# Second attention: row scaling on ScalarE, weight scaling on GpSimd, in place of one VectorE step

## The reference, cut to what matters

```
def _dyn_quant(x):
    s = jnp.maximum(jnp.max(jnp.abs(x), axis=-1, keepdims=True) / 127.0, EPS)
    q = jnp.clip(jnp.round(x / s), -127.0, 127.0)
    return (q, s)
def _w8a8_linear(x, w, b):
    qx, sx = _dyn_quant(x)
    qw, sw = _quant_weight(w)
    y = jnp.einsum('bnc,oc->bno', qx, qw) * (sx * sw[:, 0])
    return y + b
...
q = _w8a8_linear(x, wq, bq) ...
attn = jax.nn.softmax(scores, axis=-1)
o = jnp.einsum('bhnl,bhld->bhnd', attn, v)
return _w8a8_linear(o, wo, bo)
...
x = x + jnp.tanh(g_xattn[1]) * _L1_xattn_ref(_layernorm(x, axis=-1), ctx_2048, ...)
x = x + jnp.tanh(g_ffn[1]) * _L1_ffn_ref(_layernorm(x, axis=-1), ...)
```

## Time and profile before

| | before |
|---|---|
| median of 3 runs | 1870.31 us |
| range of the runs | 1869.5 to 1870.43 us |
| the profiled execution's own time | 1871.33 us |
| its span in the trace | 1869.5 us |
| PE busy | 1741.5 us (93%) |
| DVE busy | 1181.8 us (63%) |
| ACT busy | 1038.8 us (56%) |
| POOL busy | 975.1 us (52%) |

### The profile page before, as it was taken

The page is one execution under the profiler, slowest core; times in us unless marked ns, Lnnn a source line. Parts: engine busy times, 40 slices in busy tenths (PEclk is TensorE's granted clock), DMA queues, the critical chain, the costliest instruction groups (busy, mean ns, idle before and its releaser), DMA issues. The chain is left out here.

```text
span 1869.5 us, 28380 instructions
## 1 busy us (share of the span) xinstructions
PE 1741.5 (93%) x10015; PEld 1355.0 (72%) x10052; DVE 1181.8 (63%) x2415; ACT 1038.8 (56%) x2334; POOL 975.1 (52%) x864
## 2 busy tenths in 40 slices
PE   6999999999999999999998999989999778879997
PEld 4777887777877778777775888879999556634443
DVE  5666555557556776567766657634334678868885
ACT  3566666655655555545554422146665367767875
POOL 5644565445654456545541100048888356657774
PEclk9999999999999999999999999999999889999999
DMA  7111111111111111012122100167889660000000
GB/s 250 48 54 51 51 36 57 55 24 51 36 41 45 51 48 50 19 32 56 53 85 92 63 23 23 45 231 209 227 247 273 160 142 1 1 7 18 24 23 23
DMA packets 113611, 141.36 MB, mean 76 GB/s; under 512 B 38000, under 2 KB 68720, under 8 KB 113280
## 3 DMA queue, kind: packets, MB, share of 16 engines
q1 hardware_dynamic: 106304, 122.76, 21.0%
q0 software_dynamic: 7168, 16.78, 4.3%
HBM read 104.91 MB, written 29.36 MB: 72 GB/s over the span
## 5 line engine op out<-in xcount | busy, mean ns | idle before, releaser
L787 POOL TENSOR_TENSOR a_xcl<-xT,a_xch 128x512 fp32r<-128x512 f32 x64 | 87.3, 1365 | 323.4 <-ACT a_xch L571 323.4
L689 DVE TENSOR_REDUCE a_nmax<-a_S 128x1 f32<-128x192 f32 (+3 forms) x256 | 135.5, 549 | 83.0 <-PE a_S L897 82.8
L954 PE MATMUL a_A<-a_pT,a_vf 128*128 128x512 f32 x320 | 168.0, 607 | 6.5 <-ACT a_pT L592 6.5
L577 ACT ACTIVATE a_pr_odd<-a_S,a_nmax 128x320 f32<-128x320 f32 (+1 forms) x128 | 80.6, 631 | 149.9 <-DVE a_nmax L689 149.8
L120 PE MATMUL a_A<-a_wlo,a_xch 128*128 128x512 f32 x256 | 143.9, 562 | 14.0 <-DVE a_qb L750 11.4
L577 ACT ACTIVATE a_pr_even<-a_S,a_nmax 128x192 f32<-128x192 f32 (+1 forms) x128 | 67.0, 526 | 123.7 <-DVE a_nmax L689 123.4
L120 PE MATMUL a_S<-xl,xh 128*128 128x288 f32 (+3 forms) x320 | 121.8, 381 | 9.7 <-DVE xl L732 5.0
L1612 POOL TENSOR_TENSOR e_wlo<-expert_raw,e_whi 128x1408 fp32r<-128x1408 f32 x31 | 100.3, 3235 | 50.2 <-ACT e_whi L1784 48.0
L2528 PE MATMUL f_HH<-w12T,f_f_xqT 128*128 128x512 bf16 x496 | 117.5, 383 | 6.9 <-DVE f_h L2384 3.8
L714 DVE RECIPROCAL a_rec<-a_rs 128x1 f32<-128x1 f32 x256 | 41.2, 161 | 120.1 <-ACT a_pr_odd L577 67.1
L120 PE MATMUL e_GUP<-e_xgl,e_whi 128*128 128x256 f32 (+1 forms) x384 | 110.4, 287 | 4.3 <-DVE e_xgl L1840 2.7
(11 more groups left out here) (417 smaller groups left out, 5593.9 us busy)
## 6 DMA issues: line engine op xcount, KB each, us to landing
a_pw<-in_L_ffn_w_dram SPq DMA_DIRECT2D x96, 256.0 KB, 2.8
expert_raw<-in_L_ffn_w_gate_dram SPq DMA_DIRECT2D x16, 704.0 KB, 8.1
expert_raw<-in_L_ffn_w_up_dram SPq DMA_DIRECT2D x16, 704.0 KB, 9.9
expert_raw<-in_L_ffn_w_down_dram SPq DMA_DIRECT2D x16, 512.0 KB, 10.3
tern<-a_tern SPq DMA_DIRECT2D x48, 128.0 KB, 1.8
x_res<-in_x_dram SPq DMA_DIRECT2D x4, 1024.0 KB, 9.2
a_raw<-in_L_xattn_wq_dram SPq DMA_DIRECT2D x4, 1024.0 KB, 6.1
a_raw<-in_L_xattn_wo_dram SPq DMA_DIRECT2D x4, 1024.0 KB, 5.5
```

Source lines behind the costliest of these rows:

```text
L577: act.activation(pr[s % 2][:, i, 0:keys(s)], pair(s, i), ACT.Exp, bias=nmax[:, s % 2, i:i + 1], accum_out=rs[:, s % 2, i:i + 1]).then_inc( ...
L689: ve.tensor_reduce(nmax[:, s % 2, i:i + 1], pair(s, i), AX.X, ALU.max, negate=True).then_inc(s_max, 1)
L787: pool.tensor_tensor(xcl[:, t % 2], xT[:, :, tok(t)], xch[:, t % 2].bitcast(F32), ALU.subtract).then_inc(xlo_ready, 1)
L954: pe.matmul(bank, vf[:, par(t), i], pT[:, i % 2], start=i == 0, stop=False)
```

## The change

The step Y leaves the DVE. Its two factors are applied apart: ACT reads the bank QY and multiplies by the row scale `so` into y (new step Y of ACT), and POOL multiplies y by `gsw` just ahead of the addition to x (both in step A). ACT runs Y at the head of a slot, for tile t-3, where DVE ran it near the end of slot t-1 for the same tile; A moves from tile t-2 to tile t-3. PE, when it wants the bank QY, now waits for ACT's read (`y_scaled`). DVE's N waits for `y_scaled` of an older tile before it overwrites `so`, and the feed-forward layer's b waits for `x_done` of its tile.

```diff
-    ACT_ORDER = "q0 t0 i0 t1 c0 v0 k0 e0 O0"
+    ACT_ORDER = "Y0 q0 t0 i0 t1 c0 v0 k0 e0 O0"
-    DVE_ORDER = "D0 o0 M0 b0 x0 N0 Y0 m0"
+    DVE_ORDER = "D0 o0 M0 b0 x0 N0 m0"
...
-             "POOL": {"B": 2, "p": 3, "s": 0, "A": -2}}
+             "POOL": {"B": 2, "p": 3, "s": 0, "A": -3}}
...
-                16: "t0.15 fs0.0 t1.15 fq0.1 fq1.1 fs1.0 fz0.0 O0.15 fs2.0 fz1.0 fs3.0 fz2.0 fc0.2 fv0.2 fz3.0 fa0.0"}
+                16: "Y0.13 t0.15 fs0.0 t1.15 Y0.14 fq0.1 fq1.1 fs1.0 fz0.0 O0.15 fs2.0 fz1.0 fs3.0 fz2.0 Y0.15 fc0.2 fv0.2 fz3.0 fa0.0"}
...
-                 16: "A0.14 fh0.0 fh1.0 fy0.2 fh2.0 fy1.2 fh3.0 A0.15 ft0.0 fp0.2"}
+                 16: "A0.13 fh0.0 A0.14 fh1.0 fy0.2 fh2.0 fy1.2 fh3.0 A0.15 ft0.0 fp0.2"}
...
                     if name == "A":
+                        pool.wait_ge(y_scaled, s + 1)
+                        pool.tensor_tensor(y[:, u], y[:, u], gsw[:], ALU.mult).then_inc(y_ready, 1)
                         pool.wait_ge(y_ready, s + 1)
                         pool.wait_ge(biased, s + 1)
                         pool.tensor_tensor(x[:, s], x[:, s], y[:, u], ALU.add).then_inc(x_done, 1)
...
+                    if name == "Y":
+                        act.wait_ge(y_full, s + 1)
+                        if s > 1:
+                            act.wait_ge(x_done, s - 1)
+                        act.activation(y[:, u], QY[:], ACT.Identity, scale=so[:, u]).then_inc(y_scaled, 1)
...
+                        if s > 1:
+                            ve.wait_ge(y_scaled, s - 1)
                         link(ve.tensor_scalar(so[:, u], amo[:, u:u + 1], 1.0 / 127.0, FLOOR, ALU.mult, ALU.max))
...
-                    if name == "Y":
-                        ve.wait_ge(y_full, s + 1)
-                        if s > 1:
-                            ve.wait_ge(x_done, s - 1)
-                        ve.scalar_tensor_tensor(y[:, u], QY[:], so[:, u], gsw[:], ALU.mult, ALU.mult).then_inc(y_ready, 1)
...
+                        ve.wait_ge(x_done, s + 1)
                         link(ve.bn_stats(f_stats[:, u], x[:, s]))
...
-                        pe.wait_ge(qs_ready if name == "Q" else y_ready, s + 1)
+                        pe.wait_ge(qs_ready if name == "Q" else y_scaled, s + 1)
```

More of the change, by code:

```diff
@@ L2032, in attention1_ffn1_stage @@
                16: "U0.14 P0.15 Y0.14 P1.15 V0.15 fP1.0 V1.15 fT0.1 fP2.0 U0.15 fP3.0 Y0.15"}
-    ACT_JOIN = {10: "q0.12 t0.9 i0.11 t1.9 c0.13 v0.13 k0.11 G0.0 e0.10 O0.9",
[6 rows of a table removed]
-    DVE_JOIN = {13: "D0.13 o0.11 M0.13 fb0.0 x0.15 N0.12 Y0.11",
[3 rows of a table removed]
-    POOL_JOIN = {13: "B0.15 s0.13 fy0.0 A0.11 fy1.0 fp0.0",
-                 14: "s0.14 fy0.1 A0.12 fy1.1 fp0.1",
-                 15: "s0.15 A0.13",
-                 16: "A0.14 fh0.0 fh1.0 fy0.2 fh2.0 fy1.2 fh3.0 A0.15 ft0.0 fp0.2"}
+    ACT_JOIN = {10: "Y0.7 q0.12 t0.9 i0.11 t1.9 c0.13 v0.13 k0.11 G0.0 e0.10 O0.9",
[6 rows of a table added]
+    DVE_JOIN = {13: "D0.13 o0.11 M0.13 fb0.0 x0.15 N0.12",
+                14: "D0.14 o0.12 M0.14 fb0.1 N0.13 fm0.0",
+                15: "D0.15 o0.13 M0.15 fx0.0 N0.14 fm0.1",
+                16: "o0.14 fg0.0 fg1.0 N0.15 fx0.1 fg2.0 o0.15 fb0.2 fg3.0 fH0.0 fH1.0"}
+    POOL_JOIN = {13: "B0.15 s0.13 fy0.0 A0.10 fy1.0 fp0.0",
+                 14: "s0.14 fy0.1 A0.11 fy1.1 fp0.1",
+                 15: "s0.15 A0.12",
+                 16: "A0.13 fh0.0 A0.14 fh1.0 fy0.2 fh2.0 fy1.2 fh3.0 A0.15 ft0.0 fp0.2"}
     HALF = H1 // 4
@@ L2103, in attention1_ffn1_stage @@
             "q_full", "qs_ready", "q_turned", "q_copied", "sc_full", "sc_read", "max_ready", "centred", "exp_done"))
-        p_turned, p_copied, o_full, o_ready, oq_ready, oq_turned, oq_copied, y_full, y_ready = (s_.sem(n) for n in (
-            "p_turned", "p_copied", "o_full", "o_ready", "oq_ready", "oq_turned", "oq_copied", "y_full", "y_ready"))
+        p_turned, p_copied, o_full, o_ready, oq_ready, oq_turned, oq_copied, y_full, y_scaled, y_ready = (s_.sem(n) for n in (
+            "p_turned", "p_copied", "o_full", "o_ready", "oq_ready", "oq_turned", "oq_copied", "y_full", "y_scaled", "y_ready"))
         biased, x_done, turned = s_.sem("biased"), s_.sem("x_done"), s_.sem("turned")
@@ L2547, in feed @@
                         else:
-                            pe.wait_ge(y_ready, NT)
+                            pe.wait_ge(y_scaled, NT)
                         for k in range(F1 // P):
```

## The result

| | before | after |
|---|---|---|
| median | 1870.12 us (18 runs) | 1872.62 us (18 runs) |
| range of the runs | 1868.74 to 1874.98 us | 1871.64 to 1876.0 us |
| ratio to before, 95% interval | | 1.0016 [1.0009, 1.0023] |
| the profiled execution's own time, its span | 1871.33, 1869.5 us | 1872.6, 1870.8 us |
| the D of slot 3 to the end of the span | 338.96 us | 342.41 us |

The changed kernel is slower by 0.16%: 2.5 us above the kernel before, 3.4 us above the forecast of 1869.2, and 0.3 us beyond the upper end of the range. It is inside the 0.2% that I had called "no change" and beside the sign that I had given it.

A forecast was written before the change was run, and what follows sets the result against it. Plain slots were bound by a ring of waits through DVE's m, then by one through S. Terms -2.5 - 0.4 + 0.58 + 1.22 = -1.1 us gave 1869.2 us against the median 1870.31; range 1866.9 to 1872.3.

The forecast's parts named there:

- seven plain slots: Slots 3 to 9: period falls to 8.03 us, gain 0.36 us each, -2.5 us in all.
- slots 10 to 14: Five slots where the read's 0.58 us is exposed and m's 0.66 saved: -0.08 us each, -0.4 in all.
- the read ahead of c: Slot 16, ACT's read of tile 15: delays c of feed-forward tile 2 and POOL's last block, +0.58 us.
- the product ahead of t: Slot 16, POOL's product of tile 15 ahead of the powers: not covered by idle time, +1.22 us.
- the old ring without Y: Plain slots, chain of waits through m, q, t0, P1 and N: 8.39 - 0.66 = 7.73 us, no longer the longest.
- rival C: Slots 2 to 14: full 0.66 us saved in each, 8.6 us, join costs 1.8, total 1863.5; chance 0.05.
- rival A: Plain slots gain nothing because ACT closes them: 1872.1 us; chance 0.15.
- the shift: Plain slots: q starts 0.05 us after the next D; taken not to accumulate, the ring being 7.89 to 8.08 us.
- Rival D: Join: the product and the read are hidden, as t waits for something else; -2.9 us, 1867.4; chance 0.05.
- part three: Prediction's step on slots 10 to 16: -0.4 us for slots 10 to 14; in slot 16 one uncovered read, 0.58 us.
- Rival B: PE's longer gap before r, 6.55 us, costs clock: 1.0 to 2.6 us more, 1870.2 to 1871.8; chance 0.10.
- a second low stretch: Sign that would prove the forecast wrong: another stretch of low PE clock in the changed kernel's profile, no size given.

The follow-up runs named there:

- e1: Changed kernel with POOL's product and sum of tile 15 moved behind the two power steps in slot 16: 1869.83 us, ratio to before 1.0000.
- e2: Changed kernel with POOL's product and sum of tile 15 behind the power steps, and ACT's read of tile 15 later too: 1870.72 us, ratio 1.0000.
- e4: Changed kernel with unused identity transposes filling PE's waits, 11 in slot 15 and 18 in slot 16: 1871.01 us, ratio 1.0005.
- e7: Kernel before with the change for tiles 7 to 15 only: 1873.05 us, ratio 1.0014.
- e5: Kernel before with one unused ACT operation added ahead of t0 of tile 14 in slot 15: 1873.80 us, ratio 1.0019.
- e9: Changed kernel with ACT's read of output 12 moved behind t0 of tile 14 in slot 15: 1870.37 us, ratio 1.0000.
- e12: Whole change, POOL's product and sum of tile 15 behind the power steps, unused transposes in slots 15, 16, the long gap and last tile: 1866.04 us, ratio 0.9977.
- e8: Kernel before with only POOL's sum of tile 15 moved behind the two power steps in slot 16: 1869.41 us, ratio 0.9993.
- e10: Kernel before with unused PE transposes, 50 in the long gap before the feed-forward layer, 18, 4 and 9 in the last tile: 1868.09 us, ratio 0.9990.
- e11: Kernel before with the change for tiles 0 to 6, POOL's tile 15 sum late, unused transposes in slot 16, long gap, last tile: 1864.84 us, ratio 0.9970.
- e3: Changed kernel with 11 unused identity transposes filling PE's wait before the first feed-forward transpose in slot 15: 1871.12 us, ratio 1.0010.
- e6: Kernel before with the change for tiles 0 to 6 only: 1869.68 us, ratio 0.9997.

## Why the prediction was wrong

The sum of the waits came out near, in one of its terms by luck. Forecast, and measured in the trace:

| term | forecast | measured |
|---|---|---|
| seven plain slots | -2.5 | -2.25 (8.05 us a slot) |
| slots 10 to 14, up to P1 of slot 15 | -0.4 | -0.5 (-1.10 up to D15, +0.57 ahead of t0) |
| the read ahead of c | +0.58 | +0.58 |
| the product ahead of t | +1.22 | +1.34 |
| sum of the waits | -1.1 | -0.86 |
| granted clock, slots 15 and 16 | 0 | +3.14 (36.98 - 33.84) |
| from M to the end | 0 | +1.17 |

**Plain slots.** The D waits for S, the slot is 8.05 us, not the 7.73 of the old ring without Y, so rival C (0.66 a slot) and rival A (nothing) both fall. That the shift doesn't feed on itself held: q starts 0.02 us after D and N comes 4.52 after q, as before. **Slots 10 to 14** were put at -0.08 us each; they measure -0.33, -0.11, -0.69, +0.08 and -0.05. Their sum is -1.10, and it meets the forecast's -0.4 only because one more read than the five, that of output 12 in slot 15, adds 0.57: the price of the term was right by luck, its mechanism at best in part. **The read** was put at 0.58 of the queue; it took 0.57 or 0.58. By the Trainium skill, "ScalarE: Activation LUTs", section "What ACT_TABLE_LOAD costs", an activation of 512 elements with one operand per partition would take, as an estimate, 0.71 us and hold the next one for 0.61; the trace agrees within 0.04 (0.69 and 0.57 in a plain slot). **The product** was mis-sized by 0.12: I priced it as one of four independent operations in a row, 1.22 apart, but the sum needs its result, and such a pair starts 1.34 apart. Rival D (hidden in the join) falls with e1 and e2: nothing hid the product or the read.

**The step that failed** is in part three: it carries "the read's 0.58 lies on the ring through q, t0 and P1" over to the join, where "the read stands in front of t0 (1633.04)", and prices the wait that this makes on PE as time alone, with nothing for the granted clock. Rival B, the one place for the clock, sets it aside with "the gap already has its low stretch". In its place the runs show a loss of 3.14 us to low clock in slots 15 and 16 of the profile (36.98 us from D15 to M against 33.84 at full clock in e4 and e7), and 3.8 us in the median when such a wait alone is added to the kernel before (e5). The clock was looked for in one place only, the long gap before r. There it cost little: the first slot of the feed-forward layer went from 13.11 to 13.57 us, +0.46, where B had 1.0 to 2.6. The loss came two slots earlier, at a wait that the kernel before also has (1.5 us before fT0.0) and behind which the change adds 0.52 us. I had priced that wait on ACT's side and never read what PE does there: the earlier trace rows shows ACT alone. PE's rows at that place would have shown the wait of 1.56 us, right ahead of the P1 that the change delays, and a clock of 1.00 that could be lost. The list of things that would prove me wrong did have "a second low stretch"; it belonged among the rivals with a place and a price. With e5's price, about 3 to 4 us on top of the forecast of 1869.2, the case would have been 1872 to 1873.

**From M to the end**, +1.17 us: 0.46 in the first slot and 0.44 in the last, both next to low clock where PE is not filled, and of different length over the profiles of this study (12.96 to 14.11, and 11.9 to 15.0 for M to the end of the last), and 0.34 in one slot of 13.31 us for 12.97. The last is a DVE row with an idle time of 0.46 us behind DVE's own reduction, where other slots have 0.1 or less:

```profile
1793.68 0.23 DVE L2401 TENSOR_SCALAR f_ST<-f_ST,f_rooth 128x1 f32<-128x1 f32 x1 [0.46 <-DVE f_ST L2397]
```

It stands at the same tile in the kernels after, e1 to e4, e9 and e12, and not in before, e5 to e8, e10 and e11. e7 has the changed join and no stall at that tile, but one like it at 1679.50 us, 0.52 us behind DVE's own statistics, where others have 0.17, and the kernel before has such a one at 1525.93 us (0.53). So stalls of this kind stand at other places in other kernels; what they are stays open.

What stays open too is what decides whether a low stretch comes in one execution. The 18 runs of the kernel after fall in ten of 1871.6 to 1872.7 us and eight of 1873.7 to 1876.0, and the second group has a mean granted clock of 0.980 to 0.982 against 0.983 to 0.984. The profile shown is one of the first group and has both stretches, so the groups are not the executions with them and those without: there is low clock elsewhere in the program too (0.50 from 1490 to 1500 us in both profiles, before and after), and the kernel before has runs at 0.984 and at 0.986. What is shown is one end: e5 brings the stretches and 3.8 us in the median by one added operation. At the other end e9 takes back 2.25 us in the median by moving one step. That e3 and e4 work through the clock rests on one profile of each and on medians whose intervals overlap that of the kernel after. The share of executions is not shown.

## What to carry to other kernels

Price an added wait on TensorE twice: once as time, and once as a chance to lose the clock; here it stood 0.6 us of work behind another wait, and whether it needs that neighbour was not tried. Read its own rows and its granted clock at every wait that a change touches, not only at the longest one. Freeing the busiest engine gains only down to the next ring (here 0.33 of 0.66 us), so find the one slot in the trace in which that ring closes and take its length. In the last tile before a new phase the order on a helper engine can be worth more than what is moved: two tiny power steps put ahead of a product and a sum were worth 2.25 us, and idle transposes in gaps that can't be closed another 1.7.

## What the runs showed of the hardware

- A wait of 0.56 us on PE, close behind one of 1.57, was followed by 6 us at a granted clock of 0.50 (1.2 GHz) and a second low stretch a slot later, and the median was 3.8 us higher (e5). With the first of the two waits filled, by 11 transposes, the clock was up in that slot though the second wait stayed (e3, e4 and e12, one profile each); it was also up in two of the five profiles with both waits and nothing filled (e1, e7). The Trainium skill, "TensorE: Matmul & The Clock Gate", section "HAM oscillation — how this bites in real kernels", says that bursts of products with waits between them can fall back to the low clock again and again and pay for it each time; the trace agrees that it falls more than once (slots 15 and 16 of the kernel after), with waits of 0.52 to 2.38 us there, shorter than those of the page's example and than the 6.55 us one at which I had looked.
- The same wait gives different results from one execution to another: one of 2.38 us in slot 16 stands ahead of eight gate products of 1.89 us in e1, and of 3.36 in the kernel after, which runs the same steps up to there; in e6 they take 3.12 us, in the kernel before, e7 and e9 1.89.
- Transposes of the identity keep the clock up though their results are not used: 50 of them in 5.62 us, and the granted clock is 1.00 from 1655 to 1668 us, where the kernel before has 0.59 behind the gap (e10).
- On POOL a sum that needs the product before it starts 1.34 us after it (128x512, fp32, kernel after); operations of that size that don't need each other start 1.22 us apart.
